# A two-layer graph network kernel: att of the second layer transposed by VectorE and DRAM instead of TensorE

## The reference

```python
# layer 0: 4 heads of 64, softmax attention masked by adj, then Wo and bias
h = maximum(layernorm(x), 0);  x = x + attention(h, adj, Wq, Wk, Wv, Wo, bo)
# layer 1: 8 heads of 64
h = maximum(layernorm(x), 0)
m = h @ map_w.T + map_b;  sem = heads(m);  n = sem / norm(sem)
cos = einsum('bhsd,bhtd->bhst', n, n) * ~sm
cos_adj = cos > 0.1
q = heads(m @ q_w.T + q_b);  k = heads(m @ k_w.T + k_b)
p_attn = softmax(where(sm, -1e10, q k^T / 8)) * keep
adj_h = cos_adj * p_attn                      # "att": 256 x 256 for each head
Ax = einsum('hbst,hbtd->hbsd', adj_h, heads(h @ gcn_map_w.T + gcn_map_b))
out = relu((Ax @ gcn_W.T) / (adj_h.sum(-1) + 1));  x = x + heads_back(out)
```

## Time and profile before

| | |
|---|---|
| median of 3 runs | 3964.74 us (3963.68 to 3965.45) |
| the profiled execution | 3964.82 us, of which its span is 3963.0 us |
| PE busy | 3888.6 us, 98% of the span, 33104 matmuls |
| DVE busy | 2387.8 us, 60% |
| ACT busy | 1999.5 us, 50% |
| POOL busy | 1333.9 us, 34% |
| DMA | 112.83 MB, mean 28 GB/s |
| mean granted TensorE clock | 0.996 |

### The profile page before, as it was taken

One profiled execution on the slowest core, in us unless ns is written; L12 is line 12 of the kernel. 1 busy time (PEld: TensorE's weight loads), 2 busy tenths in 40 slices (PEclk: granted clock), 3 DMA queues, 4 the chain that ended last, 5 costly groups with the idle time before them and its releaser, 6 DMA issues. The chain is left out here.

```text
span 3963.0 us, 104587 instructions
## 1 busy us (share of the span) xinstructions
PE 3888.6 (98%) x33104; PEld 3442.2 (87%) x33104; DVE 2387.8 (60%) x8920; ACT 1999.5 (50%) x5587; POOL 1333.9 (34%) x2007
## 2 busy tenths in 40 slices
PE   7999999999999999999999999999999999999998
PEld 5888888888888888888888888888888888888887
DVE  3566666665665666666666656656666666666564
ACT  2455455455455454554554554554545545545544
POOL 2333333333333333333333333333333333333332
PEclk8999999999999999999999999999999999999999
DMA  3000000000000000000000000000000000000000
GB/s 89 29 17 33 33 17 33 31 18 33 28 22 33 22 27 33 17 33 33 17 33 33 17 33 28 22 33 22 27 33 17 33 33 17 33 32 18 33 28 17
DMA packets 66072, 112.83 MB, mean 28 GB/s; under 512 B 20896, under 2 KB 22464, under 8 KB 66048
## 3 DMA queue, kind: packets, MB, share of 16 engines
q1 hardware_dynamic: 65456, 111.17, 8.1%
q0 software_dynamic: 592, 1.35, 0.2%
HBM read 45.39 MB, written 33.55 MB: 20 GB/s over the span
## 5 line engine op out<-in xcount | busy, mean ns | idle before, releaser
L564 ACT ACTIVATE att<-att,nmax 128x256 f32<-128x256 f32 x1024 | 510.8, 500 | 487.6 <-DVE nmax L722 487.6
L474 POOL TENSOR_TENSOR x_res<-x_res,rel 128x256 f32<-128x256 f32 x256 | 188.9, 738 | 1096.6 <-DVE rel L749 1096.6
L722 DVE CUSTOM_DVE_ANT_0 att<-bank,mask 128x256 f32<-128x256 f32 x1024 | 382.5, 421 | 248.1 <-PE bank L929 236.5
L570 ACT ACTIVATE uT<-bank 128x512 f32<-128x512 f32 x512 | 291.7, 597 | 330.9 <-PE bank L902 330.9
L909 PE MATMUL bank<-gT,w_q 128*128 128x256 f32 x3072 | 421.7, 286 | 0.0
L909 PE MATMUL bank<-gT,w_k 128*128 128x256 f32 x3072 | 415.7, 284 | 0.0
L733 DVE SCALAR_TENSOR_TENSOR att<-bank,att 128x256 f32<-128x256 f32 x1024 | 391.3, 420 | 24.2 <-ACT att L564 18.3
L909 PE MATMUL bank<-hT,w_qkv 128*128 128x256 f32 x3072 | 397.2, 285 | 6.4 <-DVE hT L756 6.4
L917 PE MATMUL bank<-w_v,gT 128*128 128x512 f32 x1536 | 390.7, 403 | 0.0
L909 PEld LDWEIGHTS bank<-gT,w_k 128*128 128x128 f32 x3072 | 384.6, 189 | 6.0
L909 PEld LDWEIGHTS bank<-hT,w_qkv 128*128 128x128 f32 x3072 | 373.0, 189 | 15.2 <-DVE w_o L652 6.8
(11 more groups left out here) (136 smaller groups left out, 7101.0 us busy)
## 6 DMA issues: line engine op xcount, KB each, us to landing
x_in<-x SPq DMA_DIRECT2D x64, 512.0 KB, 3.3
x_res<-x_mid SPq DMA_DIRECT2D x64, 512.0 KB, 2.9
out<-x_res SPq DMA_DIRECT2D x64, 512.0 KB, 2.9
adj<-adj SPq DMA_DIRECT2D x64, 64.0 KB, 2.5
att<-gcn_map POOLq DMA_DIRECT2D x2, 512.0 KB, 9.1
att<-map_rows SPq DMA_DIRECT2D x1, 1024.0 KB, 5.2
x_mid<-wq SPq DMA_DIRECT2D x1, 512.0 KB, 6.4
x_res<-wk SPq DMA_DIRECT2D x1, 512.0 KB, 7.4
```

The lines of the kernel that those rows point to most:

```text
L474: g.tensor_tensor(part, part, rel[:, :, :], ALU.add).then_inc(res_added, 1)
L564: s_.activation(e_sl, e_sl, ACT.Exp, bias=nmax1[:, p, c, e:e + 1], scale=-1.0, accum_out=esum1[:, p, c, e:e + 1]).then_inc(exp1_done, 1)
L570: s_.activation(uT[:, e, :], t_bank[e][:, :], ACT.Copy).then_inc(uT_ready, 1)
L722: v_.tensor_tensor_reduce(out=att[:, p % 2, e, c, :], in0=score_bank[e][:, c * N:c * N + N], in1=mask1[:, c, :], scale=-SCALE, scalar=FLT_ ...
```

## The change

att of layer 1 is no longer transposed by PE. A new step "flip_a"/"flip_b" on DVE transposes each 32x32 block of a head's att in place (one operation of 128x512). SP writes each flipped head to a DRAM scratch ("spill_a", "spill_b": 128 partitions x 4 pieces of 512 bytes) and reads a pair back into uT ("shift": four DMAs, each for 32 partitions, in pieces of 1 KB), so that the blocks come to the partitions where the transposed matrix has them. The steps "turn_a" and "turn_b" of PE and ACT are gone. The layout of att is now (pair parity, block of 32 columns modulo 4, head, tile, half, 32), and the operands of "score", "cos", "value" and the masks are read or written in that order. `v_bank` is one bank (4) for "value" and "back", and the products rotate over 3 banks (5 to 7). "score" waits for the maskings of the pair before, "cos" for its gates. "value" waits for the four reads; "shift" waits for both writes and for "value" of the pair before. All five lists are written anew.

```diff
--- before.py
+++ after.py
...
     TENSOR = [
...
+        ("score", 0), "ht0a", "ht0b", ("k", 2), "qk0", "qk1", ("cos", 0), ("score", 1), "s0", "s1", ("q", 2), "qk2", "qk3",
+        ("vv", 0), "pt0", ("cos", 1), ("score", 2), "s2", "s3", ("vv", 1), "pt1", "v0", "pt2", "pt3", ("cos", 2), "av",
+        ("value", 0), ("k", 3), "wo0", ("back", 0), "wo1", ("value", 1), ("q", 3), ("back", 1), ("cos", 3), ("score", 3),
+        "ht1a", "ht1b", ("value", 2), "m0", "m1", "m2", "m3", "q0", ("back", 2), "ss", "k0", "q1", ("value", 3), "rt", "k1",
+        "bc0", "bc1", ("back", 3)
     ]
     SCALAR = [
...
+        "ht0a", "ht0b", ("unit", 0), ("k", 2), ("unit", 1), "qk0", ("exp_a", 0), "qk1", ("q", 2), "exp0", ("exp_b", 0), "qk2",
+        "qk3", ("exp_a", 1), "pt0", "exp1", ("exp_b", 1), "exp2", "pt1", "exp3", ("exp_a", 2), "pt2", "pt3", ("exp_b", 2),
+        "av", ("value", 0), ("k", 3), ("value", 1), ("q", 3), "ht1a", "ht1b", ("exp_a", 3), "m0", ("exp_b", 3), "m1", "m2",
+        ("value", 2), "m3", "q0", "k0", "q1", ("value", 3), "k1"
     ]
     VECTOR = [
...
+        "ht0a", "ht0b", ("score_a", 0), ("score_b", 0), "qk0", "qk1", ("k", 2), "s0", "s1", ("q", 2), ("cos_a", 0),
+        ("score_a", 1), ("cos_b", 0), ("flip_a", 0), "qk2", "sum0", ("score_b", 1), ("vv", 0), "qk3", ("factor", 0),
+        ("cos_a", 1), ("flip_b", 0), "s2", "sum1", "s3", ("cos_b", 1), "sum2", ("score_a", 2), "sum3", ("vv", 1),
+        ("score_b", 2), "v0", ("flip_a", 1), ("flip_b", 1), ("cos_a", 2), ("cos_b", 2), ("flip_a", 2), ("flip_b", 2), "av",
+        ("back", 0), "wo0", ("k", 3), "wo1", ("factor", 1), ("q", 3), "norm1", ("back", 1), ("factor", 2), ("score_a", 3),
+        "ht1a", "ht1b", ("cos_a", 3), ("score_b", 3), ("cos_b", 3), ("flip_a", 3), ("flip_b", 3), "stats0", ("back", 2), "q0",
+        "ss", "norm0", "k0", "q1", ("factor", 3), "rt", "bc0", "bc1", "k1", ("back", 3)
     ]
     POOL = [
...
+        ("unit", 0), "mask0", "sum0", ("unit", 1), "mid", "sum1", "sum2", "sum3", "rstd1", ("back", 0), "m0", ("back", 1),
+        "m1", "m2", "m3", "rstd0", "pow", ("back", 2), "mask1", ("back", 3)
     ]
-    PBANKS = 4
+    PBANKS = 3
     SYNC = [
-        "x", ("out", 0), "adj", "move"
+        ("spill_a", 0), ("spill_b", 0), ("shift", 0), ("spill_a", 1), "x", ("spill_b", 1), ("shift", 1), ("spill_a", 2),
+        ("spill_b", 2), ("shift", 2), ("spill_a", 3), ("spill_b", 3), ("shift", 3), "adj", ("out", 0), "move"
     ]
...
-    bank_of = {s: 4 + k % PBANKS for k, s in enumerate(PRODUCTS)}
+    bank_of = {s: 5 + k % PBANKS for k, s in enumerate(PRODUCTS)}
...
-        att = sb("att", [128, 2, 2, C, N])
+        att = sb("att", [128, 2, 4, 2, C, C, 32])
...
+        uT_blocks = uT[:, :, :].rearrange("p e n -> p (e n)").rearrange("p (r e c j f) -> p r e c j f", e=2, c=C, j=C, f=32)
...
-        score_bank, gram_bank, t_bank = bank[0:2], bank[2:4], bank[0:2]
-        v_bank = gram_bank
+        score_bank, gram_bank = bank[0:2], bank[2:4]
+        v_bank = (bank[4], bank[4])
...
+
+                        e = "ab".index(kind[6])
+                        sp.wait_ge(flipped, pairs(a, p, 2) + e + 1)
+                        sp.sem_inc(passed_sync, 1)
+                        if e == 0:
+                            sp.wait_ge(turned[(p + 2) % 4], BLOCK_MOVES * (a + (1 if p < 2 else 2)))
+                            sp.sem_inc(passed_sync, 1)
+                        sp.dma_start(scratch[p % 2, :, :, e, :], att[:, p % 2, :, e, :, :, :].rearrange("p b c j f -> p b (c j f)")).then_inc(spilled[p], 16)
+                    elif kind == "shift":
+
+                        sp.wait_ge(spilled[p], 32 * (a + 2))
+                        sp.sem_inc(passed_sync, 1)
+                        sp.wait_ge(uv_full, pairs(a, p))
+                        sp.sem_inc(passed_sync, 1)
+                        for cols in range(4):
+                            sp.dma_start(uT_blocks[32 * cols:32 * cols + 32, :, :, :, :, :].rearrange("p r e c j f -> p r (e c j f)"),
+                                         scratch[p % 2, :, cols, :, :].rearrange("(r p) e x -> p r (e x)", p=32)).then_inc(turned[p], 16)
...
+                            g.tensor_scalar(mask1[:, c, :].rearrange("p (b j f) -> p b j f", j=C, f=32),
+                                            adj8[:, c, :].rearrange("p (j b f) -> p b j f", j=C, f=32), MASKED_L1, 0.0,
+                                            ALU.mult, ALU.add).then_inc(mask1_ready, 1)
...
+                        if e == 0:
+                            dve.wait_ge(spilled[(p + 2) % 4], 32 * (a + (1 if p < 2 else 2)))
+                            dve.sem_inc(passed_vector, 1)
...
+                            v_.tensor_tensor_reduce(out=att[:, p % 2, :, e, c, :, :].rearrange("p b j f -> p b (j f)"), in0=in_blocks(score_bank[e][:, c * N:c * N + N]), in1=in_blocks(mask1[:, c, :]),
                                                     scale=-SCALE, scalar=FLT_MAX, op0=ALU.add, op1=ALU.min,
                                                     accum_out=nmax1[:, p, c, e:e + 1]).then_inc(masked, 1)
...
+                            e_sl = att[:, p % 2, :, e, c, :, :].rearrange("p b j f -> p b (j f)")
+                            v_.scalar_tensor_tensor(e_sl, in_blocks(gram_bank[e][:, c * N:c * N + N]), COS_THRESHOLD, e_sl, ALU.is_gt, ALU.mult,
                                                     accum_out=usum1[:, p, c, e:e + 1]).then_inc(gated, 1)
+                    elif kind in ("flip_a", "flip_b"):
+
+                        e = "ab".index(kind[5])
+                        dve.wait_ge(gated, pairs(a, p, 4) + 2 * e + 2)
+                        dve.sem_inc(passed_vector, 1)
+                        blocks = att[:, p % 2, :, e, :, :, :].rearrange("p b c j f -> p b (c j f)")
+                        v_.transpose(blocks, blocks).then_inc(flipped, 1)
...
+            def by_quarter(ap, source):
+
+                return ap.rearrange("p (j b f) -> p b j f", j=C, f=32) if source else ap.rearrange("p (b j f) -> p b j f", j=C, f=32)
+
+            def head_products(banks, left, right, order=lambda ap, source: ap):
...
+                            last[e] = t_.matmul(order(banks[e][:, c * N:c * N + N], False), left[r, ls, c * 128:c * 128 + 128],
+                                                order(right[r, rs, :], True), start=(i == 0), stop=(i == 2))
...
+                        last = t_.matmul(dst[64 * e:64 * e + 64, :].rearrange("p (c r f) -> p c r f", c=C, f=32), v[:, jc, (hd0 + e) * DH:(hd0 + e + 1) * DH], rhs(e, jc),
                                          start=(jc == 0), stop=(jc == C - 1))
...
-                        head_products(score_bank, q1[:, :, p % 2, :], k1[:, :, p % 2, :])[1].then_inc(score_full, 1)
+                        pe.wait_ge(masked, pairs(a, p, 4))
+                        head_products(score_bank, q1[:, :, p % 2, :], k1[:, :, p % 2, :], by_quarter)[1].then_inc(score_full, 1)
                     elif kind == "cos":
                         pe.wait_ge(nlow_done, 2 * a + 2 + p // 2 + 1)
+                        pe.wait_ge(gated, pairs(a, p, 4))
+                        head_products(gram_bank, nrm[:, :, p, :], nrm[:, :, p, :], by_quarter)[1].then_inc(gram_full, 1)
+                    elif kind == "value":
+                        pe.wait_ge(turned[p], BLOCK_MOVES * (a + 2))
                         pe.wait_ge(rel_done, pairs(a, p))
-                        head_products(gram_bank, nrm[:, :, p, :], nrm[:, :, p, :])[1].then_inc(gram_full, 1)
-                    elif kind in ("turn_a", "turn_b"):
-                        e = "ab".index(kind[5])
-                        pe.wait_ge(gated, pairs(a, p, 4) + 2 * e + 2)
-                        transposes(t_bank[e], lambda jc, c: att[:, p % 2, e, c, jc * 128:jc * 128 + 128]).then_inc(t_full, 1)
-                    elif kind == "value":
-                        pe.wait_ge(uT_ready, pairs(a, p, 2) + 2)
                         if p == 0:
                             evicted(a, "vv", 1)
-                        values(v_bank[0][:, 0:N], v1, 2 * p, lambda e, jc: uT[:, e, jc * N:jc * N + N]).then_inc(uv_full, 1)
+                        values(v_bank[0][:, 0:N], v1, 2 * p, lambda e, jc: uT_blocks[:, :, e, :, jc, :].rearrange("p r c f -> p c r f")).then_inc(uv_full, 1)
...
     args.append(nc.dram_tensor("out", arrays["x"].shape, F32, kind="ExternalOutput").ap())
+    args.append(nc.dram_tensor("scratch", (2, 128, 4, 2, 128), F32, kind="Internal").ap())
```

More of the change, by code:

```diff
@@ L19, with gnn_two_layers @@
 COS_THRESHOLD = 0.1
+BLOCK_MOVES = 64
 MASKED_L1 = -1e10
 FLT_MAX = float(np.finfo(np.float32).max)
-def gnn_two_layers(nc, x, adj, wq, wk, wv, wo, bo, map_t, map_rows, map_b, q_t, q_b, k_t, k_b, gcn_map, gcn_map_b, gcn_t, out):
+def gnn_two_layers(nc, x, adj, wq, wk, wv, wo, bo, map_t, map_rows, map_b, q_t, q_b, k_t, k_b, gcn_map, gcn_map_b, gcn_t, out, scratch):
     G, N, D = x.shape
@@ L50, in gnn_two_layers @@
     TENSOR = [
[L51 to L54, removed]
@@ L257, in gnn_two_layers @@
```

(26 more changed lines are left out.)

36 lines of the change are left out of this document (7 added, 29 removed), and 5 rows, old and new, of the table VECTOR.

## The result

The changed kernel takes 4120.9 us (median of 4 runs, 4107.07 to 4126.26), where the kernel before takes 3964.5: a ratio of 1.039, 95% interval 1.036 to 1.042. It is slower by 156 us, or 3.9%. The prediction was 3820 us, 3758 to 4005, with 0.75 on faster. It was wrong in its sign.

What follows compares the result with a forecast made beforehand. PE's in-order list was taken as the bound, busy 98% of the span. Span 3963.0 less 211 for the turns, plus 66 of waits and 1.8 around the span, gave 3820 us, range 3758 to 4005.

Steps and rivals of the forecast that it cites:

- What is removed: On PE, 2048 turns of att go, 32 a round, 3.29 us a round, 211 us over 64 rounds.
- predicted floor 3760: Rival case in which all PE waits are hidden, with about 0.1 us a round left: 3760 us, chance 0.15.
- Banks, "cos", operands in runs of 32: On PE, waits before products or "cos" cost 0.3 us together; operands read in runs of 32 cost nothing.
- The flip: On VectorE, eight in-place flips of 128x512 a round at 0.60 us each, 4.8 us a round.
- Rival 3: On VectorE, a flip costs 1.23 us, adding 2.3 us a round: 3965 us, no change; chance 0.06.
- A landing: SP transfer from issue to arrival: 2.9 us for a write, 2.6 for a read; bounds 2.5 and 3.7.
- Rival 2: DRAM round trip: small pieces make every landing 1 us longer, adding 3.3 us a round before "value": 4028 us; chance 0.18.
- Pair 1: Chain from end of v0 to "value" 1 takes 10.0 us against 9.3 of PE work: PE waits 0.7 us.
- Bandwidth: On the DMA queues, 4 MB a round, about 70 GB/s beside today's 27, meets no bandwidth limit.
- The clock: PE's granted clock, expected to be still 1.00 in the changed kernel.
- pt1: PE step needing head 1 normalised; the walk listed pt0, needing head 0 normalised by POOL, at 0.1 us.
- Pair 3: From end of score 3 to "value" 3, a chain of 13.5 us against 14.2 of PE work: just hidden.

Runs made afterwards that it cites:

- the run of order and banks alone: Changed kernel without flips, writes and reads, "value" multiplying by a constant tile; new order, three banks and block-wise operands stay: 3765.0 us.
- the filler: Changed kernel with constant-operand matmuls, results unused, added in front of "value" of pair 1: 4073.0 us with 12, 4051.5 us with 24.
- the two moves: Two separate runs against the changed kernel: flips of pair 1 before the masking of pair 2, 3914.5 us; x before both writes of pair 1, 3923.0 us.
- run 18: Not a follow-up run: in "the end of the run 18" the number is 18 us of waits in the last half round of the changed kernel.

## Why the prediction was wrong, point by point

- **What is removed: right.** 211 us for the turns, from start to start; without flips and transfers the kernel is 201 us faster than before, at 3765 us (predicted floor 3760). But "contradicts" was said too fast of the Trainium skill's 275 ns (TensorE: Matmul & The Clock Gate, Part 4: PE-mode transpose): that figure is a duration, and as a duration the trace agrees with it (274 ns in the earlier trace rows). What it doesn't give is the cost in the list, 103 ns.
- **Banks, "cos", operands in runs of 32: right.** After the start of the run no PE wait stands before a product for its bank, 12 matmuls on nrm or on k, q take 0.82 and 0.72 us from start to start in the median, and the run of order and banks alone shows no cost.
- **The flip: right.** 0.60 us taken. One lasts 0.692 us, but the two of pair 1 start at 2028.00 and the next operation at 2029.22, so in VectorE's list a flip costs 0.61. The estimate of 1.24 us from the Trainium skill's 311 ns (VectorE: DVE Perf Modes, The three transpose paths) is refuted by that row; the same page's advice to use TensorE for 128x128 turns stands in another section, Rules for kernel authors. Rival 3 did not occur.
- **A landing: right as a median, wrong where it counts.** 2.9 us taken for a write, 2.8 measured; 2.6 for a read, 2.9 measured. Rival 2 had the right place (a trip through DRAM in front of "value") but the wrong mechanism: the small pieces did not make landings in general 1 us longer. By its own terms it would also need 0.73 us more a landing to decide against the change, not 0.65.
- **Pair 1, the failed step.** The chain from the end of v0 to "value" 1 was put at 10.0 us. It takes 12.98 in the round shown and 12.5 in the median. The issue of the second write was put at 2.55 us after v0 and came at 3.50 (a write's issue takes 0.52, and x and the write behind it came 1.02 and 0.61 us apart, where 0.5 in all was allowed for). From there to the reads the sum had some 3.35 us, with an upper bound of 3.7 for which no row stood; with x ahead in the same queue it was 4.46. The reads took 4.51 instead of 4.1. So the price of the queue, with x in it, was the mis-sized term: moving x alone took 2.0 us out of the first two legs, and nothing out of the third. The forecast gave this wait 0.7 us; it is 3.2 in the mean.
- **Bandwidth: no limit shown.** "Far from what lands now" was argued from a mean of 70 GB/s. In the 4 us of the reads shown the DMA engines were 86% busy and moved 246 GB/s, as the writes of pair 2 ran beside them, and those reads took 5.10 us, the longest of all rounds. But in the median the last read of pair 1 lands 4.47 us after the first is issued, and that of pair 3, with no write beside it, after 4.52. So the traffic doesn't account for the usual wait.
- **The clock: left out.** The prediction expected 1.00. A wait of 3.68 us was followed by 4 us at 0.57. About 70 us come from this, as the filler and the two moves show.
- **pt1: 0.1 us allowed, 0.92 measured.** The walk took the three operations of the factor at their usual length and did not ask what POOL does beside them. Moving them gave 47 us.
- **Pair 3: "just hidden" by 0.7 us, 0.50 us of waiting measured.** Pair 2 was hidden, as predicted.
- **The end of the run: put at nothing.** Only 63 rounds were counted. Three waits in the last half round (5.51, 2.83 and 9.43 us) add 18 us.
- **Where it all goes.** Against the forecast of 3820, 301 us are missing. The waits before "value" 1 in the 63 rounds are 202 us instead of 63 x 0.7 = 44, which is 158 more; those of pair 3 are 30, the end of the run 18, pt1 60 less the 6 allowed, the clock 69 or more. That makes 329, an estimate; 35 are given back by waits for h and rn that were there before and are gone (21.6 and 21.8 us before, 8.3 and 0.5 after), and 294 of the 301 are accounted for.

The weakest point was the margin, not any single row: three of the four "value" steps were found within 1 us of their data, and two terms of one chain had errors of that size. The 0.21 on slower was too little for that.

## What to carry to other kernels

When work is moved from a full engine to a chain of queue, DRAM and queue, its price is read at the one place where the engine's list meets the chain: count every issue in the in-order queue and each transfer ahead in the same queue, and look at the end of the run, where nothing hides the trip. A long wait on TensorE can be paid twice, through the granted clock: here the matmuls behind it ran slow in 36 of 64 rounds at 3.2 us of waiting in the mean, and in one of 64 at 1.2 us. Before such a change is given up, the orders are worth a look: here the same change went from 3.9% slower to 3.9% faster by moving five entries of two lists.

## What the runs showed of the hardware that I had not expected

- Adding 24 matmuls (3 us of PE work) to a round made the kernel 69 us faster, because they stood in a wait and kept the clock up (0.968 to 0.993).
- The same wait of about 3 us was followed by the lower clock in some rounds and by the full one in others (36 and 28 of 64), and the longer wait wasn't always the one that was followed by it.
- A two-input VectorE operation on 4 elements took 1.15 us, 157 ns in other places, while GpSimd ran additions of 128x512; a one-input operation between two such took 0.18 us.
- 269 MB more traffic to and from DRAM, 99 GB/s instead of 29, cost nothing in itself (3843 against 3840 us).
- From the issue of a 256 KB write to that of the reads that wait for it 4.5 us passed when the write came 0.6 us behind a load of 512 KB in the same queue, and 3.4 when only its neighbour was just ahead (medians); four reads issued one after the other take 1.73 us of the queue's time.
